# The last stage of a four-layer image network: the skip path is put into two product banks, and half of the low parts moves to the vector engine

## The reference, cut to what matters

```python
def _L3_conv_ref(x, w1, w2, gamma1, beta1, mean1, var1, gamma2, beta2, mean2, var2):
    residual = x
    out = _conv3x3(x, w1, stride=1)
    out = jax.nn.relu(_bn(out, gamma1, beta1, mean1, var1))
    out = _conv3x3(out, w2, stride=1)
    out = _bn(out, gamma2, beta2, mean2, var2)
    return jax.nn.relu(out + residual)

x = x + _L3_conv_ref(_gn(x), ...)
```

## Time and profile before

| | |
|---|---|
| median of 3 runs | 3703.07 us (3700.73 to 3705.16) |
| the profiled execution | 3706.38 us |
| its span, first to last instruction | 3704.6 us |
| mean granted TensorE clock | 0.979 of full speed |
| the last layer's blocks | first matmul 3260.5 us, last 3698.6 us |
| busy in the span | PE 95%, DVE 64%, ACT 57%, POOL 45% |

### The profile page before, as it was taken

How to read it: one execution, slowest core, us unless ns; L and a number is a source line. 1 busy time by engine, 2 the same in 40 slices (tenths; PEclk the granted TensorE clock), 3 DMA queues, 4 the chain that set the end, 5 groups by cost and what they waited for, 6 DMA issues and landing times. The chain is left out here.

```text
span 3704.6 us, 102441 instructions
## 1 busy us (share of the span) xinstructions
PE 3505.9 (95%) x31974; PEld 2969.0 (80%) x31974; DVE 2367.6 (64%) x6301; ACT 2114.0 (57%) x5882; POOL 1662.5 (45%) x2589
## 2 busy tenths in 40 slices
PE   7989899999999999979999999999999969979999
PEld 4656565656566565679999999999999969979998
DVE  5868787877878786843333333343333369988898
ACT  5979797978888797944443333333333334345544
POOL 2746464646565564600013333333334446556665
PEclk9999999999999999989999999999999989989999
DMA  6232323333231414221110000000002200000000
GB/s 225 68 100 75 100 77 93 82 91 84 66 104 61 113 49 125 55 73 51 45 40 0 0 0 0 0 0 0 0 18 62 62 16 1 5 28 18 36 35 36
DMA packets 202833, 193.93 MB, mean 52 GB/s; under 512 B 35744, under 2 KB 191136, under 8 KB 199456
## 3 DMA queue, kind: packets, MB, share of 16 engines
q1 hardware_dynamic: 171168, 177.15, 15.4%
q10 hardware_dynamic: 31360, 12.87, 1.3%
HBM read 123.30 MB, written 66.58 MB: 51 GB/s over the span
## 5 line engine op out<-in xcount | busy, mean ns | idle before, releaser
L199 PE MATMUL bank<-h,w_hh 128*128 128x128 f32 x8032 | 933.8, 275 | 0.0
L199 PEld LDWEIGHTS bank<-h,w_hh 128*128 128x128 f32 x8032 | 917.0, 192 | 0.0
L244 ACT ACTIVATE h<-bank,bg 128x128 f32<-128x128 f32 x1008 | 370.0, 367 | 818.7 <-PE bank L199 818.6
L1626 ACT ACTIVATE Pr<-bank,nmx 128x256 f32<-128x256 f32 x1568 | 722.6, 477 | 101.5 <-DVE nmx L1764 82.8
L1556 POOL TENSOR_TENSOR Pr<-Pr,rden 128x768 f32<-128x768 f32 x392 | 575.5, 1468 | 382.1 <-DVE rden L1843 382.1
L1764 DVE TENSOR_REDUCE nmx<-bank 128x1 f32<-128x256 f32 x1568 | 555.8, 417 | 179.9 <-PE bank L1970 174.4
L290 DVE SCALAR_TENSOR_TENSOR inp<-bank,b_in,tz 128x256 f32<-128x256 f32 x196 | 85.8, 479 | 693.0 <-ACT tz L227 693.0
L1981 PE MATMUL bank<-ident,Pr 128*128 128x128 f32 x3136 | 463.1, 285 | 16.9 <-POOL Pr L1556 13.1
L1981 PEld LDWEIGHTS bank<-ident,Pr 128*128 128x128 f32 x3136 | 335.1, 142 | 136.5 <-POOL Pr L1556 66.4
L1548 POOL COPY kg<-kT 128x64 f32 x1568 | 307.5, 242 | 297.0 <-DMA row<-ix 242.8
L1635 ACT ACTIVATE PT<-bank 128x512 f32<-128x512 f32 x784 | 427.0, 602 | 22.9 <-PE bank L1981 20.0
(11 more groups left out here) (263 smaller groups left out, 6475.6 us busy)
## 6 DMA issues: line engine op xcount, KB each, us to landing
v_rows<-v_padded SPq DMA_DIRECT2D x168, 232.0 KB, 3.3
vg<-v_windows SPq DMA_DIRECT2D x1176, 32.0 KB, 2.1
first_gates<-gate_sums SPq DMA_DIRECT2D x28, 512.0 KB, 2.6
gate_sums<-first_gates SPq DMA_DIRECT2D x28, 512.0 KB, 3.6
v_padded<-vpad SPq DMA_DIRECT2D x56, 232.0 KB, 2.1
X<-in_x SPq DMA_DIRECT2D x8, 1568.0 KB, 15.3
vg<-v_windows ACTq DMA_DIRECT2D x392, 32.0 KB, 2.2
x_backup<-X SPq DMA_DIRECT2D x8, 1568.0 KB, 6.0
```

Source lines behind the costliest of these rows:

```text
L199: ins = pe.matmul(bank[m][:, tt * COLS:(tt + 1) * COLS], w_hh[:, k, m * 128:(m + 1) * 128], prev[:, k, :], start=False, stop=(k == NH - 1) ...
L244: act.activation(h[:, 2 * q + tt, m, :], bank[m][:, tt * COLS:(tt + 1) * COLS], ACT.Tanh, bias=bg[:, 0, m:m + 1]).then_inc(s_h, 1)
L1626: act.activation(Pr[:, par, j, :], bank[j][:, 0:KEYS], ACT.Exp, bias=nmx[:, par, j:j + 1], accum_out=den[:, par, j:j + 1])\
```

## The change

In the second convolution the skip path no longer starts in `y_ring`. ScalarE writes it into the two product banks that are read last: A*x + tb for the even pixels into bank 0, and its negative for the odd ones into bank 3 (odd output subtracts product 3), two instructions of 392 elements in `residual(q+1)`, behind `first(q)`, as soon as the outputs of turn q-1 are formed. TensorE adds its products 0 and 3 onto them (start=False, `held`), behind a wait for `s_res` ahead of each of the two. The outputs of both convolutions are now formed by the same four instructions, and `first(q)` is the copy of product 1 in all turns.

Of the low parts, GpSimd makes the first half. The second half is a VectorE instruction, `rest_lo(q+1)`, in turn q behind `last_output(q-1)` and ahead of `add_x(q-1)` and `points(q+2)`. TensorE's block q waits for both. `formed(q)` becomes 4q. Two small constants (-A and -tb) are made at the start.

```diff
+def split_product(pe, ps, w, x, first, last, held=False):
+    pe.matmul(ps, w[0], x[0], start=first, stop=False, skip_group_check=held)
...
+        ntb, nA = sb("minus_tb", [C, B]), sb("minus_scale", [C, B])
...
         def formed(q):
-            n, i, b = block_of(q)
-            return n * 10 * NRB + (4 * NRB + 6 * b if i else 4 * b)
+            return 4 * q
...
                 def lo(q):
-                    for h in range(2):
-                        pool.wait_ge(s_hi, 2 * q + h + 1)
-                        pool.tensor_tensor(halves(v[:, q % 3, 1], h), halves(pts, h),
-                                           halves(v[:, q % 3, 0], h).bitcast(F32), ALU.subtract).then_inc(s_lo, 1)
+                    pool.wait_ge(s_hi, 2 * q + 1)
+                    pool.tensor_tensor(halves(v[:, q % 3, 1], 0), halves(pts, 0),
+                                       halves(v[:, q % 3, 0], 0).bitcast(F32), ALU.subtract).then_inc(s_lo, 1)
...
                 def first(q):
                     if q >= 2 and block_of(q - 2)[1]:
                         act.wait_ge(s_f, nth(q - 2) + 1)
+                    act.wait_ge(s_m, 4 * q + 1)
+                    act.activation(yp[q % 2][:, :, 1], bank[4 * (q % 2) + 1][:, 0:PROD], ACT.Copy).then_inc(s_s1, 1)
+
+                def residual(q):
+
                     n, i, b = block_of(q)
                     if i:
-                        act.activation(y[:, q % 2], xrows(n, b), ACT.Identity, bias=tb[:, n:n + 1], scale=A[:, n:n + 1])\
-                            .then_inc(s_s1, 1)
-                    else:
-                        act.wait_ge(s_m, 4 * q + 1)
-                        act.activation(yp[q % 2][:, :, 1], bank[4 * (q % 2) + 1][:, 0:PROD], ACT.Copy).then_inc(s_s1, 1)
+                        x = xrows(n, b).rearrange("p (k e) -> p k e", e=2)
+                        act.wait_ge(s_e, formed(q - 1))
+                        act.activation(bank[4 * (q % 2)][:, 0:PROD], x[:, :, 0], ACT.Identity,
+                                       bias=tb[:, n:n + 1], scale=A[:, n:n + 1]).then_inc(s_res, 1)
+                        act.activation(bank[4 * (q % 2) + 3][:, 0:PROD], x[:, :, 1], ACT.Identity,
+                                       bias=ntb[:, n:n + 1], scale=nA[:, n:n + 1]).then_inc(s_res, 1)
...
                     first(q)
+                    if q + 1 < NQ:
+                        residual(q + 1)
...
+                dve.tensor_scalar(nA[:], A[:], -1.0, None, ALU.mult).then_inc(s_k, 1)
+                dve.wait_ge(s_k, 10)
+                dve.tensor_scalar(ntb[:], tb[:], -1.0, None, ALU.mult).then_inc(s_k, 1)
...
                     if q:
-                        dve.wait_ge(s_lo, 2 * q)
+                        dve.wait_ge(s_lor, q)
...
+                def rest_lo(q):
+
+                    dve.wait_ge(s_hi, 2 * q + 2)
+                    dve.tensor_tensor(halves(v[:, q % 3, 1], 1), halves(pts, 1),
+                                      halves(v[:, q % 3, 0], 1).bitcast(F32), ALU.subtract).then_inc(s_lor, 1)
...
                     dve.wait_ge(s_s1, q + 1)
-                    if block_of(q)[1]:
-                        dve.wait_ge(s_m, 4 * q + 1)
-                        dve.tensor_tensor(o_, ps[1], o_, ALU.add).then_inc(s_e, 1)
-                        dve.tensor_tensor(e, ps[1], e, ALU.add).then_inc(s_e, 1)
-                        dve.wait_ge(s_m, 4 * q + 2)
-                        dve.wait_ge(s_e, e0 + 1)
-                        dve.scalar_tensor_tensor(o_, ps[2], -1.0, o_, ALU.mult, ALU.add).then_inc(s_e, 1)
-                        dve.wait_ge(s_e, e0 + 2)
-                        dve.tensor_tensor(e, ps[2], e, ALU.add).then_inc(s_e, 1)
-                    else:
-                        dve.wait_ge(s_m, 4 * q + 2)
-                        dve.tensor_tensor(e, ps[2], o_, ALU.add).then_inc(s_e, 1)
-                        dve.scalar_tensor_tensor(o_, ps[2], -1.0, o_, ALU.mult, ALU.add).then_inc(s_e, 1)
+                    dve.wait_ge(s_m, 4 * q + 2)
+                    dve.tensor_tensor(e, ps[2], o_, ALU.add).then_inc(s_e, 1)
+                    dve.scalar_tensor_tensor(o_, ps[2], -1.0, o_, ALU.mult, ALU.add).then_inc(s_e, 1)
...
                 points(0)
+                rest_lo(0)
                 points(1)
+                rest_lo(1)
...
                         last_output(q - 1)
+                        if q + 1 < NQ:
+                            rest_lo(q + 1)
                         if block_of(q - 1)[1]:
                             add_x(q - 1)
...
-                    pe.wait_ge(s_lo, 2 * q + 2)
+                    pe.wait_ge(s_lo, q + 1)
+                    pe.wait_ge(s_lor, q + 1)
...
                     for j in ORDER:
+                        held = i == 1 and j in (0, 3)
+                        if held:
+                            pe.wait_ge(s_res, 2 * nth(q) + (1 if j == 0 else 2))
```

More of the change, by code:

```diff
@@ L673, in _ @@
                     pe.wait_ge(s_agg, B)
[L676 to L680, removed]
+def split_product(pe, ps, w, x, first, last, held=False):
+    pe.matmul(ps, w[0], x[0], start=first, stop=False, skip_group_check=held)
+    pe.matmul(ps, w[0], x[1], start=False, stop=False, skip_group_check=held)
+    return pe.matmul(ps, w[1], x[0], start=False, stop=last, skip_group_check=held)
 BORDERS = 4
@@ L922, in conv_pair @@
         s_z, s_pt, s_hi, s_lo = sem("z_ready"), sem("points_ready"), sem("points_hi_ready"), sem("points_lo_ready")
+        s_lor = sem("rest_of_points_lo_ready")
+        s_res = sem("residual_in_banks")
         s_m, s_s1, s_e = sem("products_ready"), sem("first_product_copied"), sem("outputs_formed")
@@ L1036, in _ @@
                 hi(1)
-                act.wait_ge(s_k, 10)
+                act.wait_ge(s_k, 12)
                 for q in range(NQ):
@@ L1075, in points @@
                     if q:
-                        dve.wait_ge(s_lo, 2 * q - 1)
+                        dve.wait_ge(s_lo, q)
                     dve.tensor_tensor(t[SLOT[0]], d[0], d[2], ALU.subtract)
@@ L1158, in _ @@
                             ins = split_product(pe, bank[4 * (q % 2) + j][:, 0:PROD], (u[i][0][:, k, :], u[i][1][:, k, :]),
-                                                (v[:, q % 3, 0, SLOT[j], at], v[:, q % 3, 1, SLOT[j], at]), dy == 0, dy == 2)
+                                                (v[:, q % 3, 0, SLOT[j], at], v[:, q % 3, 1, SLOT[j], at]),
+                                                dy == 0 and not held, dy == 2, held)
                         ins.then_inc(s_m, 1)
```

## The result

| | before | after |
|---|---|---|
| median of 4 runs, us | 3703.59 (3700.73 to 3705.16) | 3679.64 (3675.65 to 3685.63) |
| ratio, 95% interval | | 0.9938, 0.992 to 0.9955 |
| profiled execution, us (span) | 3706.38 (3704.6) | 3677.57 (3675.8) |
| P(63) - P(3), us | 406.21 | 384.00 |
| P(63) to the end of the span, us | 12.38 | 10.93 |

The changed kernel is faster by 24.0 us between the medians, 0.65%; the ratio in the table is that of the means, 0.62%. P(q) is again the start of block q's 36 matmuls.

What follows compares the result with a forecast made beforehand. The prediction took VectorE's 7.25 us second-convolution turn to set the last stage's pace against TensorE's 6.40 floor. 22.2 + 1.3 + 1.0 = 24.5 us off 3703.07 gave 3678.6 us; range for 8 in 10: 3674 to 3688.

Steps and rivals of the forecast that it cites:

- 22.2 + 1.3 + 1.0: Forecast gain in us: TensorE's gaps over blocks 3 to 62, the tail, and the start; sum 24.5.
- The floor of 6.40: Last stage: a block's 36 matmuls take TensorE 6.40 us without a gap; 60 blocks take 384.0 us.
- the 7.25: Second-convolution turn before: VectorE's instructions sum to 7.25 us without idle time, so VectorE sets the pace.
- The remaining rival, that it does nothing: Rival 4: the gaps have another cause and move elsewhere, 3703 us; chance 0.03.
- The turn after: VectorE's second-convolution turn in the changed kernel: 6.45 us against 7.25; TensorE is then the bound.
- One turn late: rest_lo for TensorE's block q+2 made in VectorE turn q+1: ready at P(q) + 8.3, wanted at P(q) + 12.8.
- ScalarE's bank writes: Two skip-path writes of 392 elements in 32 turns, each between 0.51 and 1.03 us, taken as 0.5.
- D + 6.95: Start of the next rest_lo, counted from last_output's start D in a VectorE turn; POOL ends at D + 6.8.
- Rival 1 (collision): POOL ends late and every rest_lo pays x on the shared port; 3711 us at x = 0.9; chance 0.04.
- x = 0.35: Rival 1's bound: a collision cost per rest_lo of up to 0.35 us stays hidden.
- Rival 2: Part of the gaps stay: slow ScalarE bank writes delay the high halves and POOL; 3690 us; chance 0.08.
- rival 3 (clock): Gapless TensorE gets its lower clock now and then, 1.7 us an episode; five give 3687 us; chance 0.05.

Runs made afterwards that it cites:

- e2: Kernel before with only the low parts of the change (second half on VectorE, one turn late), skip path as before: 3679.28 us, ratio 0.9925.
- e4: Changed kernel with ScalarE writing the skip path into its two banks twice, same values: 3677.03 us.
- e3: Changed kernel with VectorE's rest_lo directly behind the points of its own block instead of one turn later: 3808.46 us.
- e5: Changed kernel with the second weights split in turn 1 and GpSimd's low part of block 2 ahead of zeroing the second padded image: 3679.82 us, ratio 0.9936.
- second profile: Changed kernel, run and profiled again unchanged: 3678.17 us, ratio 0.9934.
- e1: Changed kernel with both halves of the low parts back on GpSimd, skip path kept in the banks: 3705.02 us, ratio 0.9996.
- e6: Kernel before with add_x moved behind the points of the same turn, nothing else: 3694.78 us.
- e7: Changed kernel with GpSimd's low-part instruction made twice, same values: 3774.67 us.

## Why the prediction was right, and which step failed

**The total and its terms held, the cause of the largest did not.** 24.5 us were forecast (22.2 + 1.3 + 1.0), 24.8 are in the trace of the stage (22.21 + 1.45 + 1.12), 24.0 between the medians. The floor of 6.40 held in each of 60 blocks, with the granted clock at 1.00.

**The step that failed is the cause of the 7.25.** The prediction said: "DVE has no idle time in this turn and sets the pace. PE waits for POOL only as the last link". That had it backwards. The rows of VectorE add up to 7.25 because add_x's length holds a wait for POOL that takes whatever is left over: free 0.95 elsewhere and it waits 0.94 more. The prediction had seen this wait and counted it as 0.86 that the change would remove, but kept "0.95 of the 2.08 goes" as a gain of its own. The first part of the change gains no more than the tail by itself, the second all. The same step had VectorE with "time to spare" in the first-convolution turns of before; they were about 6.38 by the ring, and the e2 kernel gets its time back there. The total came right since both theories end at the same floor: once VectorE's turns of an image add up to no more than TensorE's 51.2, it doesn't matter by how much. In this the forecast was lucky: for the skip path alone the same arithmetic gives 7.25 - 0.95 = 6.30 a turn and about 3680, and 3705.02 was measured.

**The remaining rival, that it does nothing, was argued against by "the DVE turn adds up to 7.25 without a rest".** For the skip path alone that rival came true, but for the tail. The sum of lengths was no evidence.

**The turn after, term by term** (predicted, measured): last_output 0.60, 0.49; rest_lo 1.01, 1.00; add_x 0.90, 0.88; points 2.14, 2.15; bank reads 1.13, 1.13; last part 0.67, 0.75. Sum 6.45, 6.40, of which 0.18 now is a wait for PE, placed by the row of L1119. The work is therefore about 6.2. The mis-sized term is last_output: the row of before has add_x behind it, which reads what it writes and starts after 0.60, as 3671.47 to 3672.07 still shows. rest_lo doesn't read it and starts after 0.49. A first-convolution turn was forecast to leave VectorE 0.8 idle, and it waits 0.86 for PE in it.

**One turn late** cost nothing, as the cover of 4.5 us had it: PE waits for rest_lo only twice in the stage, both times at its start. **ScalarE's bank writes** were taken at 0.5 between 0.51 and 1.03. They are 0.70 long, one term that was too small. The slack covers it: even twice the writes left 6.40.

**The margin** between POOL's end and rest_lo was given as 0.15 (D + 6.95 against D + 6.8). The D + 6.95 doesn't follow from the prediction's own terms: a turn of 6.40 to 6.45 and the 0.60 of last_output make 7.00 to 7.05. In the turn shown it is 0.10, with last_output at 0.49. Rival 1 (collision) didn't occur in the kernel after but for the first two rest_lo (2.00 and 2.02 long, ahead of the loop), against "never 2". The e4 kernel shows what some of it costs, nothing, as the bound of x = 0.35 had it (0.26 a block); e3 shows 64 collisions that do cost. Rival 2 and rival 3 (clock) didn't occur either. Only block 2, behind its gap of 1.85, still has a stretch at the lower level: 8.02 us to the next block at a mean granted clock of 0.79, as before (8.06, 0.79). The gap alone doesn't bring that: block 2 of the e4 kernel stands behind a gap of 1.35 and block 3 of the e5 kernel behind one of 1.68, both at 1.00. What decides it, no run here tells.

**The start** gained by the path the prediction gave, with rest_lo(2) as the releaser of block 2. P(3) comes 1.12 earlier, counted from tb; 1.35 in the second profile (36.29). **The tail**: the final L1119 starts 0.03 after PE's last matmul ends (3671.44), where 0.2 was the bound.

**On the Trainium skill's rule.** In e1 add_x is 2.77 long where 0.97 is its own time, and in e6 POOL's pair is 4.91 where 4.23 is. The page SBUF — State Buffer, section Who interferes with whom, says that a VectorE instruction with two SBUF inputs and a GpSimd one that reads SBUF contend for the shared port, and that the second fully blocks; the trace agrees in both directions. The e7 kernel shows that VectorE can get in between two GpSimd instructions of which the second waits for the first. The prediction drew on it to weigh a danger of the change. Its better use was to explain the kernel before: the port was a link of the ring that set the pace.

What stays open: what the room that the skip path makes on VectorE would be worth if a block had less TensorE work. No run here has that.

## What to carry to other kernels

When an engine's rows fill a turn without a gap, compare each length with the same instruction where its neighbour is idle, before you call the engine the bound: a length that is above it is a wait, and it absorbs whatever is saved elsewhere on that engine. Sum the ring through the engine that is waited for instead (here 4.22 + 0.76 + 2.27), and shorten the longest link in it, not the one who waits. Look at the short turns too: a long turn costs nothing if the engine can catch up in the others, as the e2 kernel does. An instruction that shares a resource goes where its rival is done and its inputs are ready: the same rest_lo in another place of the turn was 129 us dearer, half by the collision and half by waiting for its input.

## What was not expected of the hardware

- Blocking lasts as long as the rest of the other engine's instruction and shows as length, not as idle time: VectorE's 0.97 became 2.87, GpSimd's pair of 4.23 became 4.91 and 5.18.
- ScalarE's write of 392 elements from SBUF (every second element) to a bank took 0.70 us, against 0.51 for the copy of 392 elements the other way. Whether the target, the stride, or the scale and bias make the difference, no run here tells.
- The first weight instruction (L712) of the last stage began 3240.1 to 3248.7 us into the span, though the code ahead of it is the same in all ten profiles. A comparison of two profiled spans is thus uncertain by several us, while blocks inside the stage keep their 6.40 to 0.01.
